# A decoder layer on one Trainium2 core: values of alternate head groups in either half of a 32-row strip

## What is computed

```python
q = proj(hs, Wq, bq, S); k = proj(at, Wk, bk, T); v = proj(at, Wv, bv, T)     # 16 heads of 16
scores = clip(einsum('bhsd,bhtd->bhst', q, k) / 4, -50, 50)                    # masked to -50 where not attended
probs = softmax(scores, axis=-1)
probs = probs / (probs.sum(axis=-1, keepdims=True) + 1e-08)
ctx = einsum('bhst,bhtd->bhsd', probs, v).transpose(0, 2, 1, 3).reshape(B, S, H)
delta = residual_scale * (ctx @ Wo.T + bo)                                    # then layer norm, residual, feed-forward
```

## Time and profile before

| | |
|---|---|
| median of 3 runs | 1429.21 us (1429.08 to 1429.45) |
| the profiled execution, its own time | 1429.21 us |
| its span | 1427.4 us |
| PE busy | 1400.9 us, 98% |
| DVE busy | 1012.6 us, 71% |
| ACT busy | 717.5 us, 50% |
| POOL busy | 447.7 us, 31% |
| mean granted clock of PE | 0.996 |

### The profile page before, as it was taken

How to read it: one execution, slowest core, us unless ns; L and a number is a source line. 1 busy time by engine, 2 the same in 40 slices (tenths; PEclk the granted TensorE clock), 3 DMA queues, 4 the chain that set the end, 5 groups by cost and what they waited for, 6 DMA issues and landing times.

```text
span 1427.4 us, 55292 instructions
## 1 busy us (share of the span) xinstructions
PE 1400.9 (98%) x25249; PEld 1183.3 (83%) x25259; DVE 1012.6 (71%) x1792; ACT 717.5 (50%) x940; POOL 447.7 (31%) x401
## 2 busy tenths in 40 slices
PE   8999999999999999999999999999999999999997
PEld 6787887786788888888888888888888888888874
DVE  5677676666247778687877778687878778677776
ACT  3535445444455555555554555555554555555540
POOL 4333233222223233233333233233333243233310
PEclk9999999999999999999999999999999999999999
DMA  9000000000211122111212122111212122111100
GB/s 270 16 1 31 2 3 29 1 30 1 67 52 47 34 75 61 48 49 46 64 31 69 37 68 64 46 49 46 64 32 77 36 60 64 46 50 46 49 3 7
DMA packets 38810, 66.78 MB, mean 47 GB/s; under 512 B 3605, under 2 KB 36818, under 8 KB 38578
## 3 DMA queue, kind: packets, MB, share of 16 engines
q1 hardware_dynamic: 38578, 63.24, 15.2%
HBM read 61.40 MB, written 1.84 MB: 44 GB/s over the span
## 4 chain that ended last, share of the span: by engine, by line
PE 71%; DVE 2%; issue 0%; POOLq 0%; POOL 0%; DVEq 0%
PE proj_ps L1311 19%; PE proj_ps L1302 19%; PE score_ps L1329 14%; PE sum_ps L1349 12%; PE side_ps L1384 2%; PE side_ps L1366 2%; PE side_ps L1398 1%; PE side_ps L1391 1%; PE side_ps L1373 0%; DVE inv L1143 0%; DVE amax L1184 0%; DVE hidden L1216 0%; DVE hidden L1227 0%; DVE sig L1226 0%; DVE exps L1131 0%
## 5 line engine op out<-in xcount | busy, mean ns | idle before, releaser
L1083 ACT ACTIVATE exps<-score_ps 125x1792 f32<-125x1792 f32 x192 | 320.6, 1670 | 420.0 <-PE score_ps L1329 420.0
L1131 DVE TENSOR_SCALAR exps<-exps,top 125x896 f32<-125x896 f32 x384 | 287.0, 789 | 18.0 <-ACT exps L1083 17.5
L1329 PE MATMUL score_ps<-spread,keys 32*125 32x112 f32 x6144 | 219.1, 279 | 0.0
L1349 PEld LDWEIGHTS sum_ps<-exps,vals 125*32 125x32 f32 x12288 | 163.1, 110 | 48.8 <-issue 35.0
L1122 DVE COPY vals<-proj_ps 125x512 f32<-125x512 f32 x192 | 128.2, 687 | 99.5 <-PE proj_ps L1311 99.0
L1329 PEld LDWEIGHTS score_ps<-spread,keys 32*125 32x125 f32 x6144 | 185.0, 183 | 15.4 <-issue 0.4
L1349 PE MATMUL sum_ps<-exps,vals 125*32 125x56 f32 x12288 | 191.6, 215 | 0.0
L1026 POOL TENSOR_TENSOR low<-raw_early,high 128x500 fp32r<-128x500 f32 x64 | 100.8, 1585 | 231.2 <-PE proj_ps L1302 122.9
L1026 POOL TENSOR_TENSOR low_early<-raw_early,high_early 128x500 fp32r<-128x500 f32 x62 | 104.0, 1686 | 172.5 <-issue 96.7
L1075 ACT ACTIVATE keys<-proj_ps,b_k 128x500 f32<-128x500 f32 x192 | 130.1, 678 | 47.9 <-PE proj_ps L1302 47.9
L289 POOL TENSOR_TENSOR swapped<-swapped,sin 128x448 f32<-128x448 f32 (+1 forms) x72 | 88.6, 1232 | 133.9 <-ACT swapped L510 133.9
(11 more groups left out here) (164 smaller groups left out, 2413.4 us busy)
## 6 DMA issues: line engine op xcount, KB each, us to landing
raw_early<-in_ctxT SPq DMA_DIRECT2D x64, 500.0 KB, 4.1
raw<-in_ctxT SPq DMA_DIRECT2D x32, 500.0 KB, 3.5
w_q<-in_attn_Wq SPq DMA_DIRECT2D x4, 512.0 KB, 7.9
w_o<-in_attn_Wo SPq DMA_DIRECT2D x1, 2048.0 KB, 19.2
out<-y_out SPq DMA_DIRECT2D x16, 112.0 KB, 1.9
rows<-in_x SPq DMA_DIRECT2D x1, 1344.0 KB, 14.9
raw_early<-in_ffn_gate_wT SPq DMA_DIRECT2D x1, 1024.0 KB, 9.0
raw_early<-in_ffn_val_wT SPq DMA_DIRECT2D x1, 1024.0 KB, 5.1
```

Source lines behind the costliest of these rows:

```text
L1083: nc.scalar.activation(exps[t % 2][:, :, :, :].rearrange("p h r n -> p r h n"), score_ps[0:TILE, :, 0:2 * QW].rearrange("p r (h n) -> p r ...
L1131: nc.vector.tensor_scalar(tile, tile, LIMIT_LO, top[:, n, at:at + 1], ALU.max, ALU.min)\
L1329: ins = nc.tensor.matmul(score_ps[0:TILE, r, to:to + HE * S], keys[c % 2][32 * r:32 * r + 32, k, (at + half) * TILE:(at + half + 1) * TILE ...
L1349: ins = nc.tensor.matmul(sum_ps[32 * h:32 * h + VW, g, :], vals[c % 2][:, at + half, HJ * g + h, :], exps[t % 2][:, half, r, col:col + S], ...
```

## The change

`add_up` takes its 32 weight columns 16 columns earlier for the heads of odd groups (g = 1, 3): the ones of the head before, and then the values. In the strip of an odd group the sums come out in the upper 16 rows and the values in the lower 16. `read_sums` joins an even and the following odd group: four instructions with the 0/1 column pair `part` write `sums` (values of the even group in the first 16 rows of a strip, of the odd one in the last 16) and `totals` (the sums of the odd group in the first 16 rows, of the even one in the last 16), each of 112 columns. `divide` swaps the halves of `totals`, takes one reciprocal of 112 columns, multiplies and adds the bias. `heads`, `b_v` and `w_xo` have two groups of full rows where they had four half empty ones, and `project` has two calls where it had four. `w_xo` and `b_v` are loaded in one transfer each; the order of the rows of Wo and bv is arranged on the host as other inputs are. Steps 2 and 5 are issued behind the pieces of their slot on PE; on DVE step 5 is issued between the two values copies, and step 2 where it was (its slot has none).

```diff
+AFTER = (2, 5)
-SWAP = [HD + n % HD for n in range(2 * HD)]
+SWAP = [(n + HD) % (2 * HD) for n in range(2 * HD)]
...
-        for j in range(HJ):
-            pairs += [(self.b_v[32 * j:32 * j + HD, :], dram["xattn_bv"][j]),
-                      (self.w_xo[32 * j:32 * j + HD, :, :],
-                       dram["xattn_WoT"].rearrange("(a j d) n -> j d a n", a=HG, j=HJ)[j])]
+        pairs += [(self.b_v[:, :], dram["xattn_bv"]), (self.part[:, :], dram["c_part"]),
+                  (self.w_xo[:, :, :], dram["xattn_WoT"].rearrange("(a p) n -> p a n", p=P))]
...
             def read_sums(i, k):
+                even, odd = sum_ps[:, 0::2, :], sum_ps[:, 1::2, :]
+                chain = Chain(dve, div_step, DIVS * (2 * i + k))
                 dve.wait_ge(probs_used, NT * i + BN * (k + 1))
-                nc.vector.tensor_copy(sums[:, k, :, :], sum_ps[:, :, :]).then_inc(sums_read, 1)
+                chain.inc(nc.vector.tensor_scalar(totals[:, k, :, :], odd, part[:, 0:1], None, ALU.mult))
+                chain(nc.vector.tensor_scalar(sums[:, k, :, :], odd, part[:, 1:2], None, ALU.mult))
+                chain.inc(nc.vector.scalar_tensor_tensor(totals[:, k, :, :], even, part[:, 1:2], totals[:, k, :, :],
+                                                         ALU.mult, ALU.add))
+                chain(nc.vector.scalar_tensor_tensor(sums[:, k, :, :], even, part[:, 0:1], sums[:, k, :, :],
+                                                     ALU.mult, ALU.add))
+                nc.vector.sem_inc(sums_read, 1)
             def divide(p, k):
-                dve.wait_ge(sums_read, 2 * p + k + 1)
-                chain = Chain(dve, div_step, 6 * p + 3 * k)
-                chain(nc.vector.reciprocal(inv[:, k, :, :], sums[:, k, :, :]))
-                nc.vector.sem_inc(inv_ready, 1)
-                chain(nc.vector.stream_shuffle(inv[:, k, :, :].rearrange("p a s -> p (a s)"),
-                                               inv[:, k, :, :].rearrange("p a s -> p (a s)"), SWAP))
-                chain(nc.vector.tensor_tensor(heads[:, :, k, :], sums[:, k, :, :], inv[:, k, :, :], ALU.mult))
-                nc.vector.tensor_tensor(heads[:, :, k, :], heads[:, :, k, :],
-                                        b_v[:, :].unsqueeze(2).to_broadcast([P, HG, S]), ALU.add)\
+                chain = Chain(dve, div_step, DIVS * (2 * p + k) + READS)
+                chain(nc.vector.stream_shuffle(totals[:, k, :, :].rearrange("p a s -> p (a s)"),
+                                               totals[:, k, :, :].rearrange("p a s -> p (a s)"), SWAP))
+                chain(nc.vector.reciprocal(totals[:, k, :, :], totals[:, k, :, :]))
+                chain(nc.vector.tensor_tensor(sums[:, k, :, :], sums[:, k, :, :], totals[:, k, :, :], ALU.mult))
+                nc.vector.tensor_tensor(heads[:, :, k, :], sums[:, k, :, :],
+                                        b_v[:, :].unsqueeze(2).to_broadcast([P, HG // 2, S]), ALU.add)\
                   .then_inc(heads_ready, 1)
...
+            def value_and_ones(r, tile, head):
+                at = (tile * XH + head) * VW - (HD if head // HJ % 2 else 0)
+                return vals[r][:, :, :, :].rearrange("p t h v -> p (t h v)")[:, at:at + VW]
...
-                                sum_ps[32 * h:32 * h + VW, g, :], vals[c % 2][:, at + half, HJ * g + h, :],
+                                sum_ps[32 * h:32 * h + VW, g, :], value_and_ones(c % 2, at + half, HJ * g + h),
...
-                    for a in range(HG):
+                    for a in range(HG // 2):
                         ins = nc.tensor.matmul(side_ps[0:ROWS, 0:D], heads[:, a, :, :].rearrange("p k s -> p (k s)"),
-                                               w_xo[:, a, :], start=(a == 0), stop=(a == HG - 1))
+                                               w_xo[:, a, :], start=(a == 0), stop=(a == HG // 2 - 1))
...
-                    if t in tail:
+                    if t in tail and t not in AFTER:
                         tail[t]()
                     if not (last and c == PC - 1):
                         for p in (2 * half, 2 * half + 1):
                             piece(PC * i + c + 1, p, (c + 1) % 2)
+                    if t in tail and t in AFTER:
+                        tail[t]()
```

More of the change, by code:

```diff
@@ L47 @@
 TOTALS = (3, 7, 11)
-N_EARLY = 11 + 2 * HJ
+N_EARLY = 14
+WEIGHTS_AT = 13
 TILE = 125
@@ L60 @@
 GATES = (7, 8)
-SWAP = [HD + n % HD for n in range(2 * HD)]
+AFTER = (2, 5)
+SWAP = [(n + HD) % (2 * HD) for n in range(2 * HD)]
+READS = 4
+DIVS = 7
 VW = 2 * HD
@@ L820, in __init__ @@
         self.ident_h = sb("ident_h", [P, P], BF16)
-        self.b_v = sb("b_v", [P, HG])
-        self.w_xo = sb("w_xo", [P, HG, D])
+        self.b_v = sb("b_v", [P, HG // 2])
+        self.w_xo = sb("w_xo", [P, HG // 2, D])
+        self.part = sb("part", [P, 2])
         self.b_xo = sb("b_xo", [ROWS, D])
@@ L906, in block_b @@
         w_h, w_l, b_k, spread, top = early.w_h, early.w_l, early.b_k, early.spread, early.top
-        head_of, ident_h, b_v, w_xo, b_xo, res = early.head_of, early.ident_h, early.b_v, early.w_xo, early.b_xo, early.res
+        head_of, ident_h, b_v, w_xo, b_xo, res, part = (early.head_of, early.ident_h, early.b_v, early.w_xo,
+                                                              early.b_xo, early.res, early.part)
         ln_gamma, ln_beta, gate_b, val_b, out_b = early.ln_gamma, early.ln_beta, early.gate_b, early.val_b, early.out_b
@@ L912, in block_b @@
         exps = [sb(f"exps{n}", [TILE, 2, HR, QW]) for n in range(2)]
-        sums = sb("sums_b", [P, 2, HG, S])
-        inv = sb("inv", [P, 2, HG, S])
-        heads = sb("heads", [P, HG, 2, S])
+        sums = sb("sums_b", [P, 2, HG // 2, S])
+        totals = sb("totals", [P, 2, HG // 2, S])
+        heads = sb("heads", [P, HG // 2, 2, S])
         delta = sb("delta", [ROWS, D])
@@ L956, in block_b @@
         div_step = sem("div_step")
-        inv_ready = sem("inv_ready")
         side_ready = sem("side_ready")
@@ new lines, in read_sums @@
+                assert chain.n == READS
+            def divide(p, k):
+                chain = Chain(dve, div_step, DIVS * (2 * p + k) + READS)
[3 more added lines that the diff above has]
+                chain(nc.vector.tensor_tensor(sums[:, k, :, :], sums[:, k, :, :], totals[:, k, :, :], ALU.mult))
+                assert READS + chain.n == DIVS
+                nc.vector.tensor_tensor(heads[:, :, k, :], sums[:, k, :, :],
+                                        b_v[:, :].unsqueeze(2).to_broadcast([P, HG // 2, S]), ALU.add)\
@@ L1268, in body @@
                         divide(i, 0)
-                    if half == 1 and not (last and c == PC - 1):
-                        for q in range(2):
-                            values_copy(PC * i + c + 1, q, (c + 1) % 2)
+                    for q in range(2) if half == 1 and not (last and c == PC - 1) else ():
+                        if q == 1 and t in tail and t in AFTER:
+                            tail[t]()
+                        values_copy(PC * i + c + 1, q, (c + 1) % 2)
+                    if half == 0 and t in tail and t in AFTER:
+                        tail[t]()
                 if not first:
@@ L1477, in constants @@
         "c_causal": np.where(np.arange(S)[None, :] > pos[:, None], np.float32(-3e38), np.float32(0)).astype(np.float32),
+        "c_part": np.stack([row % (2 * HD) < HD, row % (2 * HD) >= HD], 1).astype(np.float32),
         "c_head_of": (row[:, None] // HD % HE == np.arange(HE)[None, :]).astype(np.float32),
@@ L1495 @@
         "xattn_WqT": a(L0_xattn_Wq).T, "xattn_WkT": a(L0_xattn_Wk).T, "xattn_WvT": a(L0_xattn_Wv).T,
-        "xattn_WoT": a(L0_xattn_Wo).T, "xattn_bq": a(L0_xattn_bq).reshape(DC, P).T,
+        "xattn_WoT": a(L0_xattn_Wo).T.reshape(HG // 2, 2, HJ, HD, D).transpose(0, 2, 1, 3, 4).reshape(D, D), "xattn_bq": a(L0_xattn_bq).reshape(DC, P).T,
         "xattn_bk": a(L0_xattn_bk).reshape(DC, P).T,
-        "xattn_bv": a(L0_xattn_bv).reshape(HG, HJ, HD).transpose(1, 2, 0), "xattn_bo": a(L0_xattn_bo), "xattn_gamma": a(L0_xattn_ln_gamma),
+        "xattn_bv": a(L0_xattn_bv).reshape(HG // 2, 2, HJ, HD).transpose(2, 1, 3, 0).reshape(P, HG // 2), "xattn_bo": a(L0_xattn_bo), "xattn_gamma": a(L0_xattn_ln_gamma),
         "xattn_beta": a(L0_xattn_ln_beta), "xattn_rs": a(L0_xattn_residual_scale).reshape(1),
```

## The result

The changed kernel takes 1415.76 us (median of 4 runs, 1415.37 to 1417.02) beside 1429.27 us for the kernel before (1429.08 to 1429.45): 13.5 us less, ratio 0.9907 with a 95% interval of 0.9895 to 0.9919. Forecast were 1414.5 us, 14.7 less, in a range of 1412.0 to 1418.7. The profiled execution took 1415.76 us with a span of 1414.0. One execution of the kernel before, among those run beside the later experiments, took 3224.11 us, and no median here counts it.

A forecast was written before the change was run, and what follows sets the result against it. PE's own instruction stream was taken to bound the loop, with DVE in the chain over the last 45 us. -12.8 + 0.5 - 2.4 = -14.7 us from 1429.21 us gave 1414.5 us, range 1412.0 to 1418.7.

The forecast's parts named there:

- the projection's four instructions: Closing projection on PE: eight instructions become four at 0.214 us each, -0.855 us a pair, 15 times, -12.8 us.
- Moving: Closing steps issued behind the pieces on PE: projection 0 us, two transposes +0.03 us each, +0.5 us in all.
- Reads and division: DVE, each half: four reads for one copy +0.7 us, half-wide division -1.14 us; both under PE in the loop, worth 0.
- The limits in front of them: Two DVE limits ahead of the reads, holding DVE for 3.28 us, should start sooner because they await the previous slot's division.
- The shifted windows and the loads: Odd groups' weights beginning 16 floats earlier: 0 us; w_xo and b_v in two DMAs for eight: 0 us.
- The end: After the loop: one division -1.14, heads sooner -0.4, last projection -0.85; in all -2.4 us, bounds -1.2 and -3.2.
- the heads: Behind the last sums, read +0.7 and division -1.14 bring the heads 0.4 us sooner: -0.4 us.
- 64 records of the sums: Sign of error: 64 records of PE's sums matmuls (L1349) exceeding 0.93 us would show the prediction wrong.
- The gap: Rival: each moved PE step pays a 0.20 us entry gap, 6.0 us return, 1420.5 us; chance 8%.
- the windows: Rival: shifted weight windows cost PE 0.23 us in each of 192 steps of sums, 44 us, 1458.5 us; chance 3%.
- the loop without gain: Rival: PE's freed 0.855 us becomes a wait, only the end gains, 1426.8 us; chance 3%.
- The late reads: Rival: stretched DVE reads end 3.6 us late for PE's sums in each of 15 pairs, 54 us, 1468 us; chance 3%.

The follow-up runs named there:

- the spares: Changed kernel plus seven unneeded matmuls where PE idles in slot 11 of the last loop: 1414.45 us, again 1414.62 beside the changed kernel's 1415.56.
- the shifted kernel: Kernel before with only the odd head groups' weight windows begun 16 columns earlier, division left as it was: 1429.62 us beside 1429.23.

## Why the prediction was right

- *PE bounds the loop; the projection's four instructions.* Forecast -12.8 us for -0.855 a pair. Measured 4.63 - 3.77 = 0.86 us a pair, and shown by issuing them twice, which brings back 12.97 us.
- *Moving.* Projection 0 forecast, 0 measured; transposes +0.5 forecast, +0.6 measured. With the projection this makes 12.3 us; the loop lost 12.19.
- *Reads and division.* +0.7 and -1.14 us forecast a half, under PE in the loop. Measured where they stand in the chain: 1.25 us of reads for 0.43, +0.8, and -1.2 for the first of the two divisions, -1.1 for the last. That they are free in the loop is shown by doubling the reads, and where it stops by fourfold reads. The limits in front of them came sooner, as said.
- *The shifted windows and the loads.* 0 forecast. For the windows it is shown. The loads were not tried alone, so their 0 is not shown; they lie in the first stretch, where no difference beyond its own spread appears.
- *The end.* This term was mis-sized: -2.4 forecast, -0.7 in the profiles and -1.3 by the medians. Its three parts came (the division -1.2, the heads -0.26 for 0.4, the projection 1.99 us to 1.13 in the chain, -0.86, together -2.3), and in the profile 1.6 us went to the clock. The step that failed is the silent one that PE's links in that chain are as long afterwards as in the one profile from which I read them. The half clock stood in the windows of the kernel before, at a place where it cost nothing, and I did not ask what it would cost elsewhere. That the half clock is the cost is shown by the spares, which bring the end to 46.22 us twice. That the change moved it there is not shown: in the shifted kernel, with nothing shortened, it lay at the same place. What decides its place in an execution stays open.
- *The signs.* Of those named ahead, the transposes add 0.12 us where at most 0.1 was named, and 64 records of the sums exceeded 0.93 us once, with 1.65 in the last loop. The first is part of the 0.6 us for 0.5. The second was meant as a sign of costly windows; what it shows is the half clock, since the loop has 0.93 throughout.
- *The rivals.* The gap, the windows and the loop without gain fell. The late reads are a true mechanism from which this change stays 2.8 us away (821.31 - 818.47). By the rule on the count of operations (the Trainium skill, "VectorE: DVE Perf Modes", "Rules for kernel authors") four for one should be dearer, and each operation does have its price, 324 to 334 ns measured. From the errata table of the same page of the Trainium skill one such read comes to 242 ns, an estimate; the measurement decides. For this kernel the count didn't matter, because DVE isn't the bound.

## What to carry to other kernels

Where one engine is busy for all of a loop, read prices as differences between links of its chain and multiply; the result comes within a few per cent, and where on the engine a step stands hardly matters. At the end of a kernel, where the chain changes engines, list the stretches of low clock together with the engine that holds the chain, and do so in more than one execution: here the stretch lay off the chain in one execution and under two links of PE in another, 1.6 us longer, with the same work. Spare matmuls where PE idled kept the clock full. And look for an instruction off the loop's path that is on the path in the last loop: one division, moved by a slot, was worth 3.9 us in the changed kernel, the clock's part included, beside 13.5 us for the whole change; in the kernel before it was worth 1.0 us, which is not clear of the spread.

## What the runs showed of the hardware beside this

A DVE instruction with one source in SBUF was much slower inside a split on GpSimd than ahead of one. The last instruction of step 4, which rounds rows, took 1135 ns on average before and 346 after, though nothing of it was changed:

```profile
L1192 DVE TENSOR_SCALAR xq<-z 112x256 bf16<-112x256 f32 x15 | 17.0, 1135 | 0.0
```

That was the group by form in the kernel before; in the changed one it is

```profile
L1202 DVE TENSOR_SCALAR xq<-z 112x256 bf16<-112x256 f32 x15 | 5.2, 346 | 0.0
```

In the changed kernel this instruction starts at 836.99 and the split at 837.03; before, it started at 843.49 inside a split that began at 843.28. The four reads out of PSUM in slot 1 lie inside a split as well (816.31 to 818.84) and take what those of slot 7 take. The Trainium skill ("SBUF — State Buffer", "Terms") says that DVE and GpSimd arbitrate for one pair of ports, held for a whole instruction, so that the loser waits instead of sharing. The traces agree as far as these places go: the instruction that starts before the split is fast, the one that starts inside it is 0.9 us longer, and what reads PSUM isn't touched. The two limits in front of the reads fit too: 3.28 us from 821.79, in a split that began at 821.72, and 1.27 us from 815.19, ahead of the one at 816.31. Starting inside a split is not enough to be slow, though. In the changed kernel two limits start at 837.18, inside the split of 837.03, and take their usual 1.27 us, while that split takes 3.77 us for 2.53: there the split is the one that was held up. No run tried it by itself.
